# Loading the modulation weights second, four raw buffers for the first batch's keys, and the value weights cut after the keys

## What the reference computes

```python
mod = (_silu(L0_c) @ L0_wmod).reshape(L0_c.shape[0], 6, 1, -1)
sa, ca, ga, sb, cb, gb = (mod[:, 0], mod[:, 1], mod[:, 2], mod[:, 3], mod[:, 4], mod[:, 5])
...
h = _layernorm(x, axis=-1) * (1 + ca) + sa
x = x + ga * _L0_attn_ref(h, L0_attn_wq, L0_attn_bq, L0_attn_wkv, L0_attn_bkv, L0_attn_wo)
h = _layernorm(x, axis=-1) * (1 + cb) + sb
x = x + gb * _L0_ffn_ref(h, L0_ffn_gate_w, L0_ffn_expert_w, L0_ffn_expert_b)
```

## Time and profile before

| | us |
|---|---|
| median of 3 runs | 931.91 (931.68 to 932.21) |
| span of the profiled execution, first to last instruction | 929.5 |
| median less span | 2.4 |
| PE busy in the span | 904.2 (97%) |
| DVE busy | 782.4 (84%) |
| ACT busy | 535.9 (58%) |
| POOL busy | 274.5 (30%) |

### The profile page before, as it was taken

One profiled execution on the slowest core, in us unless ns is written; L12 is line 12 of the kernel. 1 busy time (PEld: TensorE's weight loads), 2 busy tenths in 40 slices (PEclk: granted clock), 3 DMA queues, 4 the chain that ended last, 5 costly groups with the idle time before them and its releaser, 6 DMA issues.

```text
span 929.5 us, 18019 instructions
## 1 busy us (share of the span) xinstructions
PE 904.2 (97%) x5353; PEld 782.2 (84%) x5353; DVE 782.4 (84%) x1775; ACT 535.9 (58%) x1224; POOL 274.5 (30%) x346
## 2 busy tenths in 40 slices
PE   5999999999999999999999999999999999999997
PEld 4788888888888888978888888888888889767775
DVE  6677888888888888888888888888888888899996
ACT  4587666666666666655666666666666655422231
POOL 4454222222222222133322222222222212466544
PEclk9999999999999999999999999999999999999999
DMA  6000000000000000100000000000000022100000
GB/s 215 7 12 13 12 13 12 11 17 17 11 11 11 11 11 7 57 6 1 24 12 12 14 12 11 11 11 11 11 11 11 12 86 81 46 12 18 23 17 24
DMA packets 23764, 21.60 MB, mean 23 GB/s; under 512 B 1530, under 2 KB 22564, under 8 KB 23716
## 3 DMA queue, kind: packets, MB, share of 16 engines
q1 hardware_dynamic: 23652, 20.99, 7.1%
q10 hardware_dynamic: 64, 0.02, 0.0%
HBM read 18.91 MB, written 2.10 MB: 23 GB/s over the span
## 4 chain that ended last, share of the span: by engine, by line
PE 87%; DVE 7%; issue 3%; ACT 2%; POOL 1%; DMA 1%; DVEq 0%; SPq 0%; POOLq 0%; ACTq 0%
PE ps_t L701 13%; PE ps_s L596 10%; PE ps_s L598 10%; PE ps_s L597 9%; PE ps_o L596 7%; PE ps_o L598 7%; PE ps_o L597 6%; PE ps_m L596 6%; PE ps_m L598 6%; PE ps_m L597 6%; PE ps_o L711 1%; PE ps_m L937 1%; PE ps_t L596 1%; PE ps_s L681 1%; DMA wmod_sb<-in_L_wmod_dram 1%
## 5 line engine op out<-in xcount | busy, mean ns | idle before, releaser
L992 ACT ACTIVATE pt_hi<-ps_t 128x512 fp32r<-128x512 f32 (+2 forms) x320 | 170.8, 534 | 143.3 <-PE ps_t L701 143.2
L1042 ACT ACTIVATE probs<-ps_s,neg_max 128x128 f32<-128x128 f32 (+7 forms) x256 | 189.8, 742 | 78.7 <-DVE neg_max L1336 74.4
L1345 DVE TENSOR_TENSOR pt_lo<-ps_t,pt_hi 128x512 fp32r<-128x512 f32 (+2 forms) x320 | 192.5, 602 | 12.6 <-ACT pt_hi L992 7.6
L1336 DVE TENSOR_REDUCE neg_max<-ps_s 128x1 f32<-128x128 f32 (+7 forms) x256 | 192.7, 753 | 3.7
L701 PE MATMUL ps_t<-ident,probs 128*128 128x128 f32 x1152 | 188.7, 272 | 2.1 <-DVE pt_lo L1345 2.1
L483 POOL TENSOR_TENSOR q_lo<-raw,q_hi 128x512 fp32r<-128x512 f32 x60 | 77.4, 1290 | 359.1 <-ACT q_hi L992 359.1
L701 PEld LDWEIGHTS ps_t<-ident,probs 128*128 128x128 f32 x1152 | 141.7, 140 | 27.1 <-DVE pt_lo L1345 8.9
L596 PE MATMUL ps_s<-k_hi,q_lo 128*128 128x512 f32 (+2 forms) x354 | 148.8, 420 | 2.3 <-ACT probs L1042 2.3
L1383 DVE SCALAR_TENSOR_TENSOR acc<-ps_m,rsum,acc 128x256 f32<-128x256 f32 x256 | 111.6, 478 | 24.3 <-PE ps_m L598 24.3
L1330 DVE TENSOR_TENSOR ps_s<-ps_s,mask 128x128 f32<-128x128 f32 x256 | 75.8, 296 | 56.9 <-PE ps_s L598 50.1
L598 PE MATMUL ps_s<-k_hi,q_hi 128*128 128x512 f32 (+2 forms) x354 | 123.5, 349 | 0.0
(11 more groups left out here) (180 smaller groups left out, 1718.0 us busy)
## 6 DMA issues: line engine op xcount, KB each, us to landing
wq_raw<-in_L_attn_wq_dram SPq DMA_DIRECT2D x32, 128.0 KB, 2.2
wo_raw<-in_L_attn_wo_dram SPq DMA_DIRECT2D x32, 128.0 KB, 2.0
wkv_raw<-in_L_attn_wkv_dram SPq DMA_DIRECT2D x2, 1024.0 KB, 6.5
we_raw<-in_L_ffn_expert_w_dram SPq DMA_DIRECT2D x1, 2048.0 KB, 10.1
x_again<-in_L_attn_x_dram SPq DMA_DIRECT2D x2, 1024.0 KB, 9.3
out_dram<-y_out SPq DMA_DIRECT2D x16, 128.0 KB, 1.7
acc<-in_L_attn_x_dram SPq DMA_DIRECT2D x2, 512.0 KB, 3.9
wmod_sb<-in_L_wmod_dram SPq DMA_DIRECT2D x2, 512.0 KB, 8.0
```

The costliest lines, as they stand in the source:

```text
L992: return nc.scalar.activation(dst, src, ACT.Copy, scale=scale)
L1042: nc.scalar.activation(probs[par][:, prob_offset(i):prob_offset(i) + w], ps_s[:, i % 2, col:col + w], ACT.Exp, bias=neg_max[:, par, i:i + ...
L1336: nc.vector.tensor_reduce(neg_max[:, par, i:i + 1], ps_s[:, i % 2, col:col + w], AXIS_X, ALU.max, negate=True).then_inc(max_set, 1)
L1345: nc.vector.tensor_tensor(pt_lo[:, q % PT, lo:CH], ps_t[:, q % 2, lo:CH], pt_hi[:, q % PT, lo:CH].bitcast(F32), ALU.subtract).then_inc(pt_ ...
```

## The change

It has five edits. (1) SP issues the first modulation weights between the two halves of x. (2) Key units 2 and 3 of batch 0 (and 6 and 7) go to `key_raw`, two more fp32 buffers in memory that the first output tile takes later, so that units 0 to 3 have four buffers, and unit u of 4 to 7 waits for `k_cut` = u - 3 in place of u - 1. (3) POOL cuts the value weights and the first query weights after `keys_lo`, not ahead of it. (4) The value bias goes through the bank `ps_o`; it waits for `rows_set` (DVE has read that bank). (5) `modulate(1)` no longer waits for DVE's copy of the value bias; the second half of the first queries, which uses `ps_o`, does.

```diff
@@ sync
             for c in range(NC):
                 tiles = slice(c * TPC, (c + 1) * TPC)
                 sp.dma_start(xs[:, tiles, :], x_tiles[:, tiles, :]).then_inc(x_in[c], 16)
-            sp.dma_start(wmod_sb[:, :, 0:2 * E].rearrange("p k (m e) -> p k m e", e=E),
-                         wmod_v[:, :, SA:CA + 1, :]).then_inc(wmod_in[0], 16)
+                if c == 0:
+                    sp.dma_start(wmod_sb[:, :, 0:2 * E].rearrange("p k (m e) -> p k m e", e=E),
+                                 wmod_v[:, :, SA:CA + 1, :]).then_inc(wmod_in[0], 16)
...
+        key_raw = at("key_raw", [P, 2, CH], F32, o_at)
...
-        def raw_of(u):
-
+        def raw_of(b, u):
+
+            if b == 0 and u < G * NC and u % 4 >= 2:
+                return key_raw[:, u % 2, :]
             return raw[:, u % 2, :]
@@ gpsimd
                 n0 = b * HEADS
-                cut_wkv(b)
-                cut_wq(n0, 0)
+                cut_wkv(b, 0)
                 if b == 0:
                     keys_lo()
+                cut_wkv(b, 1)
+                cut_wq(n0, 0)
                 cut_wq(n0 + 1, 1)
@@ tensor
                         if u == 2:
 
-                            pe.matmul(ps_m[:, :], ones_row[0:1, :], vb_row[0:1, :], start=True,
+                            pe.wait_ge(rows_set, 1)
+                            pe.matmul(ps_o[:, :], ones_row[0:1, :], vb_row[0:1, :], start=True,
                                       stop=True).then_inc(vb_mm, 1)
                         if u == 4:
-                            pe.wait_ge(vb_set, 1)
                             modulate(1)
...
                 if b > 0:
                     pe.wait_ge(o_lo_set, n0 * NC)
+                else:
+                    pe.wait_ge(vb_set, 1)
                 queries(n0, 0, b, 1, ps_o)
@@ vector
-                if 2 <= u < G * NC:
+                if b == 0 and 2 <= u < 4:
+                    pass
+                elif b == 0 and 4 <= u < G * NC:
+                    dve.wait_ge(k_cut, u - 3)
+                elif 2 <= u < G * NC:
                     dve.wait_ge(k_cut, G * NC * b + u - 1)
```

More of the change, by code:

```diff
@@ L413, in _, with cut_wkv @@
                 inverse_deviations(c * TPC, (c + 1) * TPC, c + 1)
[L415 to L420, removed]
+            def cut_wkv(b, i):
+                hi, lo = ((wk_hi, wk_lo), (wv_hi, wv_lo))[i]
+                for k in range(KE):
+                    pool.wait_ge(wkv_hi_set, 4 * b + 2 * i + k + 1)
+                    pool.tensor_tensor(lo[:, k, :, :], wkv_raw[:, k, :, i, :], hi[:, k, :, :].bitcast(F32),
+                                       ALU.subtract).then_inc(wkv_lo_set, 1)
             def clear_sums(b):
@@ L431, in keys_lo @@
                     pool.wait_ge(kv_hi, u + 1)
-                    pool.tensor_tensor(k_lo[:, g, part], raw_of(u), k_hi[:, g, part].bitcast(F32),
+                    pool.tensor_tensor(k_lo[:, g, part], raw_of(0, u), k_hi[:, g, part].bitcast(F32),
                                        ALU.subtract).then_inc(k_cut, 1)
@@ L443, in values_lo @@
                         continue
-                    pool.tensor_tensor(v_lo[:, j, :, :].rearrange("p g d -> p (g d)"), raw_of(G * NC + j),
+                    pool.tensor_tensor(v_lo[:, j, :, :].rearrange("p g d -> p (g d)"), raw_of(b, G * NC + j),
                                        v_hi[:, j, :, :].rearrange("p g d -> p (g d)").bitcast(F32),
@@ L1115, in upper @@
                     if b == 0 and u < KEYS_POOL:
-                        keep_hi(raw_of(u), raw_of(u), SCALE).then_inc(k_scaled, 1)
+                        keep_hi(raw_of(b, u), raw_of(b, u), SCALE).then_inc(k_scaled, 1)
                         act.wait_ge(k_scaled, u + 1)
@@ L1120, in upper @@
                     if c == 0:
-                        keep_hi(k_whole[:, g, :], raw_of(u)[:, 0:P], scale)
-                    keep_hi(k_hi[:, g, c * CH:(c + 1) * CH], raw_of(u), scale).then_inc(kv_hi, 1)
+                        keep_hi(k_whole[:, g, :], raw_of(b, u)[:, 0:P], scale)
+                    keep_hi(k_hi[:, g, c * CH:(c + 1) * CH], raw_of(b, u), scale).then_inc(kv_hi, 1)
                 else:
@@ L1125, in upper @@
                     if j + 1 < NT:
-                        last = keep_hi(v_hi[:, j, :, :].rearrange("p g d -> p (g d)"), raw_of(u))
+                        last = keep_hi(v_hi[:, j, :, :].rearrange("p g d -> p (g d)"), raw_of(b, u))
                     if j % TPC + 1 == TPC:
-                        last = keep_hi(v_whole[:, j // TPC, :, :].rearrange("p g d -> p (g d)"), raw_of(u))
+                        last = keep_hi(v_whole[:, j // TPC, :, :].rearrange("p g d -> p (g d)"), raw_of(b, u))
                     last.then_inc(kv_hi, 1)
@@ L1301, in kv_raw_part @@
                     c, g = divmod(u, G)
-                    last = nc.vector.scalar_tensor_tensor(raw_of(u), kv_bank(u),
+                    last = nc.vector.scalar_tensor_tensor(raw_of(b, u), kv_bank(u),
                                                           qk_bias[:, HEADS + g:HEADS + g + 1],
@@ L1305, in kv_raw_part @@
                 else:
-                    last = nc.vector.tensor_tensor(raw_of(u), ps_t[:, u % 2, :], v_bias[:, :], ALU.add)
+                    last = nc.vector.tensor_tensor(raw_of(b, u), ps_t[:, u % 2, :], v_bias[:, :], ALU.add)
                 last.then_inc(kv_raw, 1)
@@ L1321, in keys_lo @@
                 dve.wait_ge(kv_hi, 16 * b + u + 1)
-                nc.vector.scalar_tensor_tensor(k_lo[:, g, part], raw_of(u), SCALE, k_hi[:, g, part].bitcast(F32),
+                nc.vector.scalar_tensor_tensor(k_lo[:, g, part], raw_of(b, u), SCALE, k_hi[:, g, part].bitcast(F32),
                                                ALU.mult, ALU.subtract).then_inc(k_cut, 1)
@@ L1535, in _ @@
                             dve.wait_ge(vb_mm, 1)
-                            nc.vector.tensor_copy(v_bias[:, :], ps_m[:, :]).then_inc(vb_set, 1)
+                            nc.vector.tensor_copy(v_bias[:, :], ps_o[:, :]).then_inc(vb_set, 1)
                         if u == 5:
```

## The result

The changed kernel takes 933.87 us in the median of 20 executions, the kernel before 931.6: 2.3 us more. The ratio on record is 1.0021 (95% interval 1.0015 to 1.0027); it is an estimate of its own and not the quotient of the two medians, which is 1.0024.

The account below looks back on a forecast made before the run. PE bounds the kernel, the change acting only up to the first queries. POOL's query weights at 35.4 to 36.8 plus 1.6 us, against 37.62, gave +0.7: span 930.2, plus 2.4 around it, 932.6 us; range 930.6 to 934.2.

Parts of the forecast that it names:

- Loads, +0.95: Start: x's second half lands later, its normalisation meets POOL's wk_lo; second turn to first key in raw +0.95 us.
- Four buffers, offset +0.4, POOL's fourth cut by 29.97: Keys: DVE's third key no longer waits 0.57 us, offset stays +0.4; POOL's four cuts end by 29.97.
- POOL's order, 35.4 without and 36.8 with two cuts ahead: First query weights: POOL ends them at 35.4, or 36.8 if two DVE k_lo cuts get in ahead; PE waits.
- modulate(1) and the value bias, covered by POOL: Keys on PE: saves 0.85 and about 1.6 us, keys end between 32.7 and 34.6; POOL covers it, gain nothing.
- From the queries' start 1.6 us to VectorE, and a full clock: First queries: 1.36 us of matmuls and about 0.2 to drain, 1.6 us until DVE takes them.
- rival B: First queries: the clock falls under them while PE idles, 1.6 us on top of 0.7, 934.2 us; chance 0.15.
- Queries at a granted 0.50: First queries: running at a granted 0.50 was listed as a sign that the forecast is wrong.
- the forecast's 38.3: First queries: DVE takes them out near 38.3, listed as a sign that the forecast is right.
- That all is handed on: After the first queries: a long PE-bound stretch hands on the start's win or loss almost whole; from 62 us only a shift.
- Rival A: End of the keys: DVE's cuts fall between POOL's instructions, collision costs nothing, 35.4 holds, 931.3 us; chance 0.24.
- rival C: Start: x's second half is hardly later, landing near 6.2 as before; -2.8 us, 929.1 us; chance 0.07.

Follow-up runs that it names:

- e5: Changed kernel, but VectorE's k_lo of batch 0 reads the product in PSUM in place of raw (one SBUF input): 932.37 us, +0.2 against the kernel before.
- e11: Changed kernel with VectorE's k_lo of batch 0 read from PSUM, again, on the same chip as a2_after: 931.82 us, +0.7 against the kernel before.
- e2: Changed kernel with the old order of the loads (both halves of x, then the modulation weights): 932.79 us, +1.1 against the kernel before.
- e3: Changed kernel with both old orders (loads and GpSimd), leaving the four buffers and the value bias in its other bank: 930.01 us, -1.6 against before.
- a2_after: The changed kernel itself, unaltered, run once more on another chip: 933.01 us, +1.9 against the kernel before.
- e7_pool_only: Kernel before with the new GpSimd order alone (two raw buffers, old loads, value bias as it was): 932.47 us, +0.3 against before.
- e10_columns_last: Changed kernel with both old orders, and VectorE normalising x's second half ahead of the copy of the modulation columns: 929.40 us, -1.8 against before.
- e6_loads_only: Kernel before with the new order of the loads alone: 932.38 us, +0.2 against before.
- e8: Changed kernel with old loads, first query weights cut ahead of the keys and value weights behind: 930.96 us, -0.2 against the kernel before.

## Why the prediction was right or wrong

The measured 933.87 lies in the range of 930.6 to 934.2 and on the side that I forecast, but it is +2.3 and not +0.7.

*Loads, +0.95.* Right: 20.88 for the first key, 19.93 before. The mechanism is as told: the normalisation has 1.9 us on top of its 1.37 beside two `wk_lo` and ends at 15.91. What reaches the end is 0.84 on one chip with the four buffers and the old GpSimd order, and 0.2, give or take 0.8, on the kernel before.

*Four buffers, offset +0.4, POOL's fourth cut by 29.97.* Right: it ended at 30.06.

*POOL's order, 35.4 without and 36.8 with two cuts ahead.* Right: 36.94. e5, e11 and e2 show both parts, the order and the lockout (5.32 us for 3.77 us of POOL's work, 1.55 where I had 1.4).

*modulate(1) and the value bias, covered by POOL.* Right in the changed kernel; uncovered in e3, together with the buffers, they are worth 1.6 us, a part of which is the half clock that the keys no longer have.

*From the queries' start 1.6 us to VectorE, and a full clock, with rival B at 0.15.* **This is the term that was mis-sized.** I made "the clock falls under the first queries" a rival where it was about as likely as not, once POOL's end was put at 36.8 and the keys' end at 32.7 to 34.6. By their mean clock about half of the executions of the changed kernel do it, and it goes with 1.3 to 1.4 us more there (3.04 against 1.77 us from the queries' start to their exit, 934.6 against 933.2), close to the 1.6 of the working. A forecast of two equal cases would have been near +1.5. Queries at a granted 0.50 was also one of the signs of being wrong that I had listed, and the profiled execution shows it. That the time still lies in the range is owed to the range taking in rival B's price. The condition that I gave B, keys that end more than 2.8 us ahead, doesn't tell the cases apart: the same kernel kept its clock after 2.89 us (a2_after) and lost it after 3.84.

*The rest.* The executions at the full clock are still 933.2, 1.6 over the kernel before, where I had 0.7. A part of it is that x landed at 8.30 to 9.0 us in eight traces with the new loads, 8.6 in the mean, where I took 8.35; that is 0.25. Another part stands in the first keys, which I took as unchanged. In the trace before, TensorE's fifth matmul of the keys is already a fast one:

```profile
19.16 0.40 PE L597 MATMUL ps_s<-h_lo,wk_hi 128*128 128x512 f32 x1
```

In a2_after the sixth is still slow, and VectorE waits for the product:

```profile
20.92 0.63 PE L604 MATMUL ps_s<-h_hi,wk_hi 128*128 128x512 f32 x1
...
21.69 0.75 DVE L1314 SCALAR_TENSOR_TENSOR raw<-ps_s,qk_bias,pos 128x512 f32<-128x512 f32 x1 [0.57 <-PE ps_s L604]
```

0.63 us is what such a matmul takes where the granted clock is 0.50; the windows show 1.00 over both of these stretches, so only the durations tell them apart. From the second turn to the first key are 4.91 to 4.93 us in three traces (before, after, e7_pool_only) and 5.38 to 5.39 in ten (all others but e10_columns_last, whose order differs). The three are just those whose granted clock falls to 0.50 between 29 and 40 us. So in these traces an execution that escapes the fall under keys or queries has paid 0.46 us at the first keys, and my sum, made from one trace of the other kind, has that at nothing. In a2_after the queries leave at 39.03, 0.7 after the forecast's 38.3: POOL ends at 37.11 (36.8 in the sum), TensorE starts 0.15 after it, and 1.77 us follow (1.6 in the sum). That is about the size of what is missing, in one trace and not as a measured median, so the exact split stays open. Nor is the half clock in the kernel before hidden: with the same order from the first key on, the queries leave 17.7 us after that key in its trace, and 16.4 in e6_loads_only at the full clock.

*That all is handed on.* Right: from the first queries out to the end of the span are 891.9 us before, 892.3 after, and 891.3 to 892.5 in the twelve other traces.

Rival A (no collision) is refuted by e11 and e8, rival C by x at 8.33.

## What to carry to other kernels

Moving work back on an engine that runs far ahead is free only up to the time at which the next engine would ask for it: write down that end with every instruction now ahead of it before taking the move as hidden, and do it again with the other edits in place, since a shorter neighbour chain takes the cover away (0.3 us became 2.8). On VectorE and GpSimd, overlap in time is not free where VectorE's instruction reads two tensors from SBUF (`k_lo`: up to 1.75 us in place of 0.68), and it wasn't for the normalisation of x either (3.27 in place of 1.37): two cuts of 2.5 us on GpSimd that nobody waited for cost 1.3 us on VectorE's side. And where a change leaves TensorE idle right before work that all wait for (2.89 to 3.84 us here), reckon with the half clock under that work as one of two even cases (10 of 20 executions here), not as a tail. And read a forecast's base from more than one trace: here the trace of the kernel before held a half clock under its keys and a faster start of them, and e6_loads_only, with the same keys, had neither.

## What the hardware showed that was not expected

The load of the modulation weights, issued third in the old order, let TensorE start at 8.24 to 10.04 us in six traces of kernels that issue it so, all else being equal up to there: a start-up time taken from one trace is good to no better than a microsecond. TensorE's idle time of 3.84 us was followed by a granted 0.50 and times of 2.89, 2.76 and 1.80 us by 1.00, in one trace each. A VectorE instruction on 8 columns took 0.60 us beside GpSimd's cut and 0.16 before. The first keys came 4.9 us after the second turn in exactly the three traces whose granted clock later fell to 0.50, and 5.4 us after it in the ten others with the same order there.
